# Heads gathered and gates spread by DMA in a one-core transformer block

## The chip, the cores and the metric

One core of a Trainium2 chip runs the whole block. TensorE (PE) does matmuls and transposes, VectorE (DVE), ScalarE (ACT) and GpSimd (POOL) the elementwise work, SyncE (SP) issues most transfers. The metric is the device time of one execution in microseconds (us), lower is better.

## The reference

Post-norm attention and a mixture of experts over 2 x 1024 tokens of 128 features, all in float32: 16 heads of 8 features, a rotation of queries and keys, a causal softmax, and then 4 experts of 512 hidden features, of which each token's two best are weighted by their gates.

```python
x = L0_attn_x                                    # (2, 1024, 128)
x = _layernorm(x + _L0_attn_ref(x, qw, kw, vw, ow))
x = _layernorm(x + _L0_ffn_ref(x, router_w, router_b, w1, w3, w2))
...
score = jnp.einsum('bhqd,bhkd->bhqk', Q, K) / scale      # Q, K after rope; causal mask
weights = jax.nn.softmax(score, axis=-1)
attn = jnp.einsum('bhqk,bhkd->bhqd', weights, V)
...
h = jax.nn.silu(jnp.einsum('td,edf->etf', xf, w1)) * jnp.einsum('td,edf->etf', xf, w3)
expert_out = jnp.einsum('etf,efd->etd', h, w2)
out = jnp.einsum('te,etd->td', gates, expert_out)        # gates: softmax over the top 2
```

## The kernel before

**Tiling.** Attention runs in 8 groups (2 batches x 4 groups of `GH` = 4 heads). A group has 1024 queries in `NC` = 2 halves `c` of `CH` = 512. Tokens are also cut in `CHUNKS` = 4 chunks of 512 for the second part of the block. Each group passes twice over its scores: first the 40 score units `S` (queries on partitions), whose rows DVE reduces to maxima, then the 20 units `T` (keys on partitions), which ACT exponentiates into `num`, and the 12 products `PV` with the values, which collect in `o_bank`.

**Stages.** Nine stages overlap two groups: `PROLOGUE` (projections, S of group 0), `FIRST`, six times `STEADY`, and `LAST`. Stage s does S of group s and T and PV of group s - 1. The order of units within a stage is a string written by hand (`STEADY_ORDER`, `FIRST_ORDER`): s, t, p are units, m is `MROWS`, n is `NORM`. Every engine walks the same plan in that order.

- `MROWS`: POOL splits the maxima into three bfloat16 parts, PE transposes them to rows (L1273), DVE casts the rows to `max_rows` (L973), SP sends them into `q_op` (L462). The T units of that half wait for them.
- `OCOPY`: ACT copies `o_bank` to `o_sb` (L775). Each head has 32 rows there: 8 features, the denominator, unused rows.
- `NORM`: PE transposes the copy, 4 instructions (L1283), DVE takes reciprocals of the denominators, 16 a partition (L980), and multiplies them in (L983), into `merged`.

S, MROWS and NORM share a ring of three PSUM banks (`job_bank`); the semaphore `job_read` counts what DVE has read.

**Between.** For each chunk, `between(ch, r)` has 15 steps r: `merged` is copied to `mg_w` and transposed (L1309, r = 0), copied to `mg_t`, multiplied with `wo` (L1314, r = 1), added to x (`resid`), normalised (r = 2 to 5), transposed, split in two parts, and the router's gates are worked out (r = 8 to 14). For chunk 0 these steps stand in `LAST` (the `C` steps), for the others among the experts' steps.

**Experts.** `experts(ch, n)` has a step n for each of 16 hidden tiles (4 experts x 4): PE makes both products of the tile (6 matmuls, L1338), ACT the silu, DVE the product `hid` (L1104), ACT and POOL the split into two parts, and PE multiplies tile n - 3 with w2 (3 matmuls, L1351). After each expert ACT copies the sum (`eo_sb`, L843), PE transposes it to tokens (L1360) and DVE adds it with the gate, 4 instructions (L1125). `between` of the next chunk runs at step n - `HEAD`, `HEAD` = 7. A product for tile n may start when `hid` of tile n - 2 is done. The end of the last chunk is layer norm, half of it on POOL (L668), and two stores.

**Queues.** Each engine works strictly in its written order. A wait in one step holds all that is behind it. SP's queue holds the loads and stores of `q_scratch` and `k_scratch`, the rows of maxima, weights and results; ACT's holds two loads of `k_op` in the prologue.

## Time and profile before

| | us |
|---|---|
| median of 3 runs | 411.76 (411.66 to 412.97) |
| profiled execution | 413.73 |
| its span, first to last instruction | 412.0 |
| PE / DVE / ACT / POOL busy in it | 386.8 / 310.0 / 260.8 / 208.2 |

The profile is of one execution, 1.97 us above the median, of which 1.73 us lie outside its span. The span falls into the prologue (0 to 45 us), FIRST (to 79.5), six steady stages of 25.64 us, LAST (234 to 256.7, its score-free part from 231.7), and four expert chunks of up to 37.83 us. Busy time of PE is modelled and contains waits that its pipeline hides; the chain of waits shows what PE was held by.

### The profile page before, as it was taken

The page shows a single profiled execution, that of the slowest core. Times are in us where ns is not written, and L with a number is a line of the kernel's source. Part 1 is how long each engine was busy: PE and PEld are TensorE (multiplying, and loading weights), DVE is VectorE, ACT ScalarE, POOL GpSimd, SP SyncE. Part 2 cuts the span into 40 slices and gives each one's busy share as a digit, 9 for nine tenths or more (in the row PEclk, how much of TensorE's full clock was granted, in tenths as well). Part 3 has the DMA queues.
Part 4 walks back from the last instruction along what each step waited for, and adds up shares of the span by engine and source line. Part 5 has one row for each costly group of instructions (what it writes and reads, how often), then busy time and mean ns, then how long its engine had stood idle before and what let it go on. Part 6 is the DMA issues. An engine that isn't in the chain of part 4 may idle for free.

```text
span 412.0 us, 7446 instructions
## 1 busy us (share of the span) xinstructions
PE 386.8 (94%) x2402; PEld 203.3 (49%) x2424; DVE 310.0 (75%) x1022; ACT 260.8 (63%) x373; POOL 208.2 (51%) x274
## 2 busy tenths in 40 slices
PE   6897979999999999999999998999999999999992
PEld 2441232323323233232332434888888888888780
DVE  2869799899999999999999761455586568656653
ACT  1361527686866868668686687666566756666560
POOL 7177478542614436044360422756476546755662
PEclk9996889999999999999999999999999999999997
DMA  7474011375232232322310000000000000000000
GB/s 233 160 216 95 0 22 29 88 237 173 55 94 45 47 82 55 95 45 46 85 27 3 3 1 2 0 2 1 2 1 25 2 1 27 2 0 2 25 2 25
DMA packets 46164, 21.14 MB, mean 51 GB/s; under 512 B 30379, under 2 KB 44331, under 8 KB 46126
## 3 DMA queue, kind: packets, MB, share of 16 engines
q1 hardware_dynamic: 42718, 18.44, 17.1%
q10 hardware_dynamic: 3408, 2.23, 1.8%
q8 instruction: 20, 0.33, 0.3%
q14 instruction: 18, 0.15, 0.1%
HBM read 13.11 MB, written 7.35 MB: 50 GB/s over the span
## 4 chain that ended last, share of the span: by engine, by line
PE 80%; DVE 10%; ACT 3%; issue 3%; DMA 2%; POOL 1%; POOLq 0%; SPq 0%; ACTq 0%; DVEq 0%
PE o_bank L1264 16%; PE bank L1338 11%; PE t_bank L1338 11%; PE bank L1223 10%; PE t_bank L1351 10%; PE t_bank L1246 8%; PE small_bank L1223 5%; DVE maxima L960 2%; DVE x_w L956 2%; PE o_bank L1360 2%; PE t_bank L1176 2%; ACT num L766 1%; DVE mg_w L956 1%; DMA wqk<-in_kw 1%; DVE mg_t L956 1%
## 5 line engine op out<-in xcount | busy, mean ns | idle before, releaser
L766 ACT ACTIVATE num<-t_bank 128x1024 f32<-128x1024 f32 (+2 forms) x160 | 141.9, 940 | 65.3 <-PE t_bank L1246 65.2
L659 POOL TENSOR_TENSOR hid_lo<-num,q_op 128x512 fp32r<-128x512 f32 x63 | 81.8, 1302 | 57.7 <-ACT q_op L830 56.5
L621 POOL TENSOR_SCALAR_AFFINE_SELECT num<-num 128x512 f32<-128x512 f32 x64 | 40.2, 638 | 102.2 <-ACT num L766 101.9
L1264 PE MATMUL o_bank<-num,v_op 128*32 128x512 f32 (+3 forms) x768 | 80.1, 497 | 0.1
L1223 PE MATMUL bank<-k_op,q_op 128*128 128x512 bf16 (+7 forms) x241 | 65.3, 327 | 3.4 <-DVE maxima L956 1.3
L830 ACT ACTIVATE q_op<-num 128x512 fp32r<-128x512 f32 x64 | 40.5, 632 | 42.6 <-DVE num L1104 42.1
L960 DVE TENSOR_REDUCE maxima<-bank 128x1 f32<-128x512 f32 x83 | 55.3, 684 | 2.0 <-PE bank L1223 0.8
L1246 PE MATMUL t_bank<-q_op,k_op 64*128 64x512 bf16 (+3 forms) x384 | 49.4, 334 | 3.7 <-ACT num L766 1.3
L1104 DVE TENSOR_TENSOR num<-bank,num 128x512 f32<-128x512 f32 x32 | 22.1, 691 | 34.3 <-ACT num L837 34.0
L1223 PEld LDWEIGHTS bank<-k_op,q_op 128*128 128x128 bf16 x257 | 20.7, 98 | 53.9 <-DVE maxima L960 21.8
L1104 DVE TENSOR_TENSOR num<-t_bank,num 128x512 f32<-128x512 f32 x32 | 22.1, 690 | 26.3 <-ACT num L837 24.0
L956 DVE CUSTOM_DVE_ANT_0 mg_w<-bank,resid 128x256 f32<-128x256 f32 (+7 forms) x94 | 39.4, 440 | 2.9 <-PE bank L1223 2.3
L1223 PE MATMUL small_bank<-k_op,q_op 128*128 128x512 bf16 (+7 forms) x121 | 36.8, 331 | 2.6 <-DVE maxima L960 1.0
L956 DVE CUSTOM_DVE_ANT_0 x_w<-small_bank,resid 128x384 f32<-128x384 f32 (+7 forms) x82 | 35.7, 453 | 4.1 <-PE small_bank L1223 2.7
L956 DVE CUSTOM_DVE_ANT_0 mg_t<-bank,resid 128x448 f32<-128x448 f32 (+7 forms) x80 | 35.8, 464 | 2.6 <-PE small_bank L1223 1.4
L960 DVE TENSOR_REDUCE maxima<-small_bank 128x1 f32<-128x512 f32 x45 | 30.8, 684 | 1.7 <-PE small_bank L1223 0.9
L1246 PEld LDWEIGHTS t_bank<-q_op,k_op 64*128 64x128 bf16 x384 | 14.0, 94 | 34.1 <-ACT num L766 16.2
L1264 PEld LDWEIGHTS o_bank<-num,v_op 128*32 128x32 f32 x768 | 16.0, 108 | 25.2 <-issue 21.5
L1338 PE MATMUL bank<-q_op,w_hi 128*128 128x512 f32 x64 | 26.8, 419 | 0.4 <-DVE num L1104 0.2
L1338 PE MATMUL t_bank<-q_op,w_hi 128*128 128x512 f32 x64 | 25.7, 402 | 0.0
L1351 PE MATMUL t_bank<-hid_lo,w_hi 128*128 128x512 f32 x64 | 25.4, 397 | 0.1
L1223 PEld LDWEIGHTS small_bank<-k_op,q_op 128*128 128x128 bf16 x127 | 11.0, 97 | 29.1 <-DVE maxima L960 11.2
(162 smaller groups left out, 654.6 us busy)
## 6 DMA issues: line engine op xcount, KB each, us to landing
q_op<-q_scratch SPq DMA_DIRECT2D x64, 48.0 KB
w_raw<-in_w_all SPq DMA_DIRECT2D x6, 512.0 KB, 4.0
k_op<-k_scratch SPq DMA_DIRECT2D x28, 96.0 KB, 2.2
xT<-in_x_feat SPq DMA_DIRECT2D x4, 256.0 KB, 6.0
x_res<-in_x_tok ACTq DMA_DIRECT2D x4, 256.0 KB, 3.1
q_scratch<-num SPq DMA_DIRECT2D x2, 384.0 KB, 2.8
k_scratch<-num SPq DMA_DIRECT2D x2, 384.0 KB, 2.9
out_tokens<-num SPq DMA_DIRECT2D x3, 256.0 KB, 2.3
```

The lines of the kernel that those rows point to most:

```text
L621: pool.affine_select(out=tile, in_=tile, compare_op=ALU.is_ge, fill=0.0, base=0, pattern=[[0, GH], [1, P]], channel_multiplier=-1)\
L659: pool.tensor_tensor(hid_lo[:, m % HB, :], hid[:, m % HB, :], hid_hi[:, m % HB, :].bitcast(F32), ALU.subtract).then_inc(f_lo, 1)
L766: act.activation(num[:, t % PB, :, off:CH].rearrange("p (k i) t -> p i k t", i=2)[:, :, h:h + each, :], t_bank[k % TB][:, :, 0:each * (CH ...
L830: act.activation(hid_hi[:, m % HB, :], hid[:, m % HB, :], ACT.Copy).then_inc(f_hi, 1)
L956: ins = dve.tensor_tensor_reduce(masked_s[job % SB][:, at], ring(s, step)[:, at], causal[:, CH - width:CH], 1.0, LOWEST, ALU.add, ALU.max, ...
L960: ins = dve.tensor_reduce(maxima[:, half, pr, j:j + 1], ring(s, step)[:, at], AX.X, ALU.max)
L1104: dve.tensor_tensor(hid[:, n % HB, :], bank[2 * (n % 2) + 1][:, :], silu_sb[:, n % 2, :], ALU.mult).then_inc(f_hid, 1)
L1223: ins = pe.matmul(ring(s, step)[:, i * width:(i + 1) * width], q_op[u][:, c, pr * NB + j % NB, :, :].rearrange("p i q -> p (i q)"), k_op[u ...
L1246: ins = pe.matmul(t_bank[k % TB][:, i, (pr - h) * width:(pr - h + 1) * width] .rearrange("p (j q) -> p j q", q=QB), k_op[w][rows, pr, kt * ...
L1264: ins = pe.matmul(o_bank[h * QD:(h + 1) * QD, off:CH], v_op[w][:, kt, h, :], num[:, t % PB, h, off:CH], start=kt == 0, stop=kt == TI * (c ...
L1338: ins = pe.matmul(bank[2 * (n % 2) + w][:, :], ws[:, at], xs[ch], start=k == 0, stop=k == 2)
L1351: ins = pe.matmul(bank[4 + e % 2][:, :], ws[:, at], hs[:, m % HB, :], start=f == 0 and k == 0, stop=f == FT - 1 and k == 2)
```

## The change

- **Heads.** `NORM` is gone. The value operand carries 8 columns of ones instead of one, so each head has its denominator on 8 rows. After both halves of a group, SP issues 8 transfers (`gather_heads`, 8 rows x 1024 each) that put the heads' features into `o_all` (the storage of `xT`) and the denominators into `den_all`, both with features on partitions.
- **Between, r = 0.** DVE takes the reciprocal of `den_all` (128 x 512) in place and multiplies `o_all` with it into `mg_t`. The copies to `mg_w` and `mg_t` and the transposes L1309 are gone, and so is the copy of the normalised x (`c_store`).
- **Gates.** SP writes the gates of a chunk to DRAM (4 transfers of 128 x 4 single floats) and reads them back as rows on all partitions (`gate_rows`, 128 x 4 x 512 floats). DVE multiplies each expert's sum with its row and adds it to `sum_t`, features on partitions. PE transposes once a chunk instead of after each expert. Statistics and the last normalisation read PSUM; POOL's share and ACT's copies go.
- **Rows of maxima** are cast by ACT, not DVE.
- **Order.** New strings for FIRST and STEADY. `between` of the next chunk stands at step n - 3 (`NEXT_AT`), not n - 7.
- **Prologue.** qw is loaded on SP's queue first, PE waits for each weight apart, a third warm matmul, projection 5 moved behind two scores, the sums of turned parts 2 and 3 on DVE, not POOL, the loads of `k_op` on SP, and the second half of group 1's loads behind the first rows of maxima.

```diff
-STEADY_ORDER = "ssmttssspssttsspssttsspsstspsttssspmsttsssptsspssttssspssttsspssttsspsnttnpp"
-FIRST_ORDER = "ssssmssssnsssststsstsstsssttsspssttsspmsttssspssttsspssttsspssnttppp"
+STEADY_ORDER = "sssmttssspsttssspssttsspstsstspssttsspssttsspmstsstsspssttsspsssttpssttppp"
+FIRST_ORDER = "ssssmsssssssststsstsstsssttsspssttsspmsttssspssttsspssttsspssttppp"
...
+NEXT_AT = E_LAST
+def next_steps(n, i):
+    r = n - NEXT_AT
+    return [(i + 1 + r // UNITS, r % UNITS)] if i + 1 + r // UNITS < CHUNKS else []
...
 SP:
             send_rows(0, next(step for step in PROLOGUE if step[0] == "MROWS"), 0)
+            load_q(sp, 1, 1, 1)
+            load_k(sp, 1, 1, 1)
...
+            def gather_heads(n):
+                b, g = divmod(n, NG)
+                sp.wait_ge(o_copied, 1 + NC * (n + 1))
+                for h in range(GH):
+                    for k, dst in enumerate((o_all, den_all)):
+                        at, rows = g * QD + h * DH, h * QD + k * DH
+                        sp.dma_start(dst[at:at + DH, b * S:(b + 1) * S], o_sb[rows:rows + DH, :])\
+                            .then_inc(heads_in[b], 16)
...
                         send_rows(s, step, u if step[1] == 0 else v)
+                        if step[1] == NC - 1 and n > 0:
+                            gather_heads(n - 1)
...
+            def spread_gates(ch):
+                cols = slice(ch * CH, (ch + 1) * CH)
+                sp.wait_ge(c_done, 1 + 2 * ch + 2)
+                for e in range(E):
+                    sp.dma_start(g_dram[e, cols].rearrange("(t p) -> p t", p=P),
+                                 gates[:, ch * TI:(ch + 1) * TI, e:e + 1].rearrange("p t e -> p (t e)"),
+                                 allow_slow_non_contiguous=True)\
+                        .then_inc(g_stored, 16)
+                sp.wait_ge(g_stored, 16 * E * (ch + 1))
+                sp.dma_start(gate_rows[ch % 2][:, :, :], g_dram[:, cols].partition_broadcast(P))\
+                    .then_inc(g_loaded[ch % 2], 16)
...
 ACT:
+                    if step[0] == "MROWS":
+                        _, c, use = step
+                        act.wait_ge(job_ready, JOB[n + 1, step] + 1)
+                        act.activation(max_rows[c][:, :], ring(n + 1, step)[0:NPR * PARTS * NB, 0:P], ACT.Copy)\
+                            .then_inc(rows_cast, 1)
...
+                        if g > 0 and c == 0:
+                            act.wait_ge(heads_in[(g - 1) // NG], 16 * 2 * GH * ((g - 1) % NG + 1))
+                        act.activation(o_sb[:, c * CH:(c + 1) * CH], o_bank[:, :], ACT.Copy).then_inc(o_copied, 1)
...
 DVE:
-                if first and r == 0:
-                    dve.wait_ge(job_read, SB + LAST_JOBS)
-                    dve.wait_ge(c_mgt, 1 + ch)
-                    dve.tensor_copy(mg_w[:, :].rearrange("p (i g r) -> p i g r", i=TI, g=NG),
-                                    merged[:, 1:1 + NG, 0:TI, :].rearrange("p g i r -> p i g r")).then_inc(c_mg, 1)
...
+                if r == 0:
+                    b, at = ch // NC, slice(ch * CH, (ch + 1) * CH)
+                    dve.wait_ge(heads_in[b], 16 * 2 * GH * NG)
                     dve.wait_ge(c_y, 1 + ch)
+                    dve.reciprocal(den_all[:, at], den_all[:, at]).then_inc(c_mg, 1)
+                    dve.wait_ge(c_mg, ch + 1)
+                    dve.tensor_tensor(mg_t[:, :], o_all[:, at], den_all[:, at], ALU.mult).then_inc(c_mgs, 1)
...
+                    if e == 0:
+                        dve.wait_ge(g_loaded[ch % 2], 16 * (ch // 2 + 1))
+                        dve.wait_ge(c_x1s, ch + 1)
+                    dve.wait_ge(f_w2, ch * UNITS + FT * (e + 1) + HB)
+                    for k, half in enumerate(halves(ch, e)):
+                        dve.tensor_tensor(gated[:, e % 2, half], bank[4 + e % 2][:, half], gate_rows[ch % 2][:, e, half],
+                                          ALU.mult).then_inc(f_eo, 1)
...
+                        dve.tensor_tensor(sum_t[:, half], gated[:, e % 2, half], (sum_t if e else x1_tw)[:, half],
+                                          ALU.add).then_inc(f_y, 1)
...
 PE:
-            for _ in range(WARM):
-                pe.matmul(o_bank[:, 0:CH - QB], causal[:, 0:P], causal[:, 0:CH - QB], start=True, stop=True)
+            for width in WARM:
+                pe.matmul(o_bank[:, 0:width], causal[:, 0:P], causal[:, 0:width], start=True, stop=True)
...
-                if r == 1:
-                    pe.wait_ge(c_mgs, 1 + ch + 1)
+                if r == 1:
+                    pe.wait_ge(c_mgs, ch + 1)
+                    pe.wait_ge(c_top, 1 + ch)
...
+                if n == TR_STEP:
+                    pe.wait_ge(f_z, ch + 1)
+                    for k, half in enumerate(halves(ch, E - 1)):
+                        pe.wait_ge(f_y, (ch + 1) * E + k)
```

How instructions move is shown at three places. The first is PE where a steady stage ends and the next begins, before (`bank`, `small_bank`: scores, rows or norms; `t_bank`: T; `o_bank`: PV):

```order
L1223 MATMUL small_bank<-k_op1,q_op1 128x512
L1283 MATMUL bank0<-ident,o_sb1 128x128 x4
L1246 MATMUL t_bank0<-q_op1,k_op1 128x512 x2
L1246 MATMUL t_bank1<-q_op1,k_op1 128x512 x2
L1283 MATMUL bank1<-ident,o_sb0 128x128 x4
L1264 MATMUL o_bank<-num,v_op0 32x256 x4
L1264 MATMUL o_bank<-num,v_op0 32x128 x4
L1223 MATMUL small_bank<-k_op0,q_op0 128x64 x2
L1223 MATMUL bank0<-k_op0,q_op0 128x128 x2
L1273 MATMUL bank1<-ident_b,max_part1 48x128
```

PE at the same place in the changed kernel:

```order
L1225 MATMUL bank1<-k_op1,q_op1 128x512
L1248 MATMUL t_bank0<-q_op1,k_op1 128x512 x2
L1248 MATMUL t_bank1<-q_op1,k_op1 128x512 x2
L1266 MATMUL o_bank<-num,v_op0 32x384 x4
L1266 MATMUL o_bank<-num,v_op0 32x256 x4
L1266 MATMUL o_bank<-num,v_op0 32x128 x4
L1225 MATMUL small_bank<-k_op0,q_op0 128x64 x2
L1225 MATMUL bank0<-k_op0,q_op0 128x128 x2
L1225 MATMUL bank1<-k_op0,q_op0 128x192 x2
L1277 MATMUL small_bank<-ident_b,max_part1 48x128
```

The eight transposes of `o_sb` are gone, and the rows of maxima stand one score unit later. The second place is DVE in the first expert chunk of the changed kernel, from `hid` of tile 3 on (`num<-bank1,num` and `num<-t_bank0,num` are `hid`):

```order
L1094 TENSOR_TENSOR num<-t_bank0,num 128x512
L1026 RECIPROCAL den_all<-den_all 128x512
L1028 TENSOR_TENSOR mg_t<-xT,den_all 128x512
L1094 TENSOR_TENSOR num<-bank1,num 128x512
L1031 TENSOR_TENSOR resid<-small_bank,x_res 128x512
L1094 TENSOR_TENSOR num<-t_bank0,num 128x512
```

The reciprocal and the product stand between `hid` of tile 3 and of tile 4; before, DVE had only `hid` there and a small norm. The third place is PE in the same chunk, step n = 4, in the changed kernel:

```order
L1324 MATMUL bank1<-q_op0,w_lo 128x512
L1337 MATMUL t_bank1<-q_op1,w_hi 128x512
L1337 MATMUL t_bank1<-q_op1,w_lo 128x512
L1337 MATMUL t_bank1<-hid_lo,w_hi 128x512
L1300 MATMUL small_bank<-wo,mg_t 128x128 x4
L1324 MATMUL t_bank0<-q_op0,w_hi 128x512
```

The product with `wo`, which reads `mg_t`, now stands between the matmuls of steps 4 and 5; before, it stood behind step 8, and the transposes of `mg_w` behind step 7.

## Rows read from the trace of the kernel before

**Rows 1.** The page, part 2: busy tenths in 40 slices.
```profile
PE   6897979999999999999999998999999999999992
DVE  2869799899999999999999761455586568656653
```

**Rows 2.** Table of stretches: start:end, length, busy us (instructions) by engine, granted clock.
```profile
133.18:158.82 25.64, 25.14 (x203) 8.16 (x210) 24.09 (x88) 19.34 (x24) 9.92 (x20) 1.00 0.28 65
...
288.95:326.78 37.83, 37.83 (x188) 31.11 (x186) 25.07 (x76) 24.03 (x42) 22.73 (x19) 1.00 0.03 8
```

**Rows 3.** Chain of waits, 133.18 to 158.82 us: shares, then start, length, what.
```profile
by line: PE o_bank L1264 36.1%; PE bank L1223 23.6%; PE t_bank L1246 18.2%; PE small_bank L1223 11.6%; DVE mg_w L956 2.4%; PE bank L1283 2.3%; PE small_bank L1283 1.7%; issue 1.4%; DVE max_rows L973 1.1%; PE bank L1273 0.8%; PE small_bank L
...
152.48 0.44 PE small_bank L1283 x4
...
153.46 0.59 PE bank L1283 x4
```

**Rows 4.** Instructions of DVE in order of time, same stage.
```profile
140.48 0.28 DVE L973 CAST max_rows<-small_bank 48x128 bf16<-48x128 f32 x1
...
153.40 0.25 DVE L980 RECIPROCAL rden<-small_bank 128x16 f32<-128x16 f32 x1
153.69 0.29 DVE L983 TENSOR_TENSOR merged<-small_bank,rden 128x128 f32<-128x128 f32 x1
```

**Rows 5.** Chain of waits, 288.95 to 326.78 us.
```profile
by line: PE bank L1338 29.6%; PE t_bank L1338 29.3%; PE t_bank L1351 29.3%; PE o_bank L1360 4.9%; PE small_bank L1314 2.4%; PE small_bank L1325 2.1%; PE small_bank L1309 1.5%; PE small_bank L1320 1.2%
...
306.93 0.44 PE o_bank L1360 x4
307.37 0.57 PE small_bank L1309 x4
```

**Rows 6.** Groups of instructions: line engine operation shapes xcount | busy, mean ns | idle before.
```profile
L980 DVE RECIPROCAL rden<-small_bank 128x16 f32<-128x16 f32 x8 | 2.0, 253 | 0.5 <-PE small_bank L1283 0.3
...
L1070 DVE TENSOR_TENSOR logits<-small_bank,rb 128x16 f32<-128x16 f32 x3 | 0.5, 162 | 0.0
```

**Rows 7.** Instructions of DVE in order of time, first chunk of the experts.
```profile
261.56 0.69 DVE L1104 TENSOR_TENSOR num<-t_bank,num 128x512 f32<-128x512 f32 x1 [0.70 <-ACT num L837]
```

**Rows 8.** Chain of waits around the same point.
```profile
258.34 0.44 PE small_bank L1283 x4
...
262.29 0.70 PE t_bank L1351 x3
```

**Rows 9.** Instructions of DVE at the start of the last attention stage.
```profile
230.24 0.17 DVE L966 TENSOR_TENSOR maxima<-maxima 128x16 f32<-128x16 f32 x1
```

**Rows 10.** Chain of waits, last attention stage.
```profile
233.91 1.16 PE bank L1314 x8
```

**Rows 11.** Chain of waits at the end of the kernel.
```profile
404.28 1.14 DVE num L1125 x4
...
408.93 0.79 POOL num L668
```

**Rows 12.** The page, parts 3 and 6: DMA queue and DMA issues with KB and us to landing.
```profile
q1 hardware_dynamic: 42718, 18.44, 17.1%
...
w_raw<-in_w_all SPq DMA_DIRECT2D x6, 512.0 KB, 4.0
...
x_res<-in_x_tok ACTq DMA_DIRECT2D x4, 256.0 KB, 3.1
```

**Rows 13.** Instructions of SP's queue in order of time: start, length, transfer.
```profile
36.85 1.63 SPq L462 DMA_DIRECT2D q_op<-max_rows  x2
38.52 0.43 SPq L470 DMA_DIRECT2D wo<-in_ow  x1
```

**Rows 14.** Table of stretches of 1 us; the last number but two is the granted clock.
```profile
31.00:32.00 1.00, 0.40 (x2) 0.10 (x1) 1.00 (x3) 0.74 (x2) 0.57 (x1) 1.00 1.00 192
32.00:33.00 1.00, 0.54 (x2) 0.10 (x1) 1.00 (x5) 0.00 (x0) 0.20 (x1) 1.00 0.88 143
33.00:34.00 1.00, 0.23 (x2) 0.11 (x2) 1.00 (x5) 0.00 (x0) 0.70 (x5) 1.00 0.77 169
...
35.00:36.00 1.00, 0.69 (x4) 0.18 (x3) 1.00 (x2) 0.00 (x0) 0.94 (x2) 0.50 0.34 51
...
44.00:45.00 1.00, 1.00 (x7) 0.24 (x5) 0.99 (x3) 0.75 (x1) 0.34 (x1) 0.50 0.00 0
```

374 lines of the change are left out of this document (152 added, 222 removed).

## The prediction

> **What bounds the kernel now.** I read the page's busy tenths first [rows 1]: PE stands at 9 from 25 us to the end, and DVE falls from 9 to about 5 where the experts begin. The two long parts therefore have different second limits, and I took a stretch of each [rows 2]: a steady stage has PE 25.14 and DVE 24.09 busy of 25.64 us, an expert chunk PE 37.83 of 37.83 and DVE only 25.07. Busy is not bound, so the chains come next. In the steady stage [rows 3] the shares of PE's lines add up to about 95%; DVE's `mg_w` and `max_rows` make 3.5%. In the expert chunk [rows 5] every listed share is PE's. So an instruction taken off PE pays in full in both, one taken off DVE pays in the experts nothing, and DVE may grow there by some 10 us a chunk, if it grows at a place where PE doesn't wait. The granted clock was 1.00 in both stretches.
>
> **Steady stages (6).** PE loses the transposes of `NORM`: 2.3 + 1.7 = 4.0% of 25.64 = 1.03 us a stage [rows 3]. DVE loses, for each half, the reciprocal and product (0.25 + 0.29) and the cast of the rows (0.28) [rows 4]: 1.6 us a stage; of the chain DVE had 3.5%, 0.9 us, part of which goes with it. ACT takes the casts, 2 x 0.25 (estimate from DVE's 0.28) on 19.34: no limit [rows 2]. SP gets 8 transfers, at 0.43 us an issue [rows 13] 3.4 us a stage; the next copy into `o_sb` waits for them, and has, by the written order, some 8 us. It is covered; were it not, ACT would hold T, and PE with it. Between -1.03 (PE's part alone) and -1.9 (with DVE's part of the chain) I take -1.45: **-8.7** for six. FIRST has one such stage: **-1.4**.
>
> **Prologue.** qw comes first, sums on DVE take 0.69, as for that size [rows 7], in place of a slower POOL, and SP sends the rows of maxima at 36.85, 2 us after their cast ended, behind loads [rows 13]; these now stand behind. PE is at the lower level of the clock until 45 us in any case [rows 14]. Nothing in the rows fixes what is late next: 0 to -3.5, taken **-1.5**.
>
> **LAST.** The product with `wo` of chunk 0 ran at 233.91 [rows 10], fed by merges already done; now it needs DVE's large reciprocal and product behind the join of maxima, which ends at 230.41 [rows 9]. With the price below, 3.4 + 0.7 after it is 234.5: 0.6 late. The norms are gone from the same stretch. **0** (-2 to +1.5). The norm behind the attention, 0.44 in the experts [rows 8], goes: **-0.4**.
>
> **Expert chunks, PE's part.** Of four groups of transposes of `eo_sb` a chunk one stays: 3 x 0.44 x 4 = -5.3. The transposes of `mg_w` go in chunks 1 to 3: 0.44 + 2 x 0.57 = 1.6, the row being 0.57 [rows 5]. Together **-6.9**. DVE's four weighted additions of about 1.14 [rows 11] become four pairs of 128 x 512 at about 1.3: +1. With the reciprocal and product (4.1) it comes to 28 to 30 of 36 us, and ACT falls: no bound by its share.
>
> **The large reciprocal.** This is the unknown, and the place counts. The trace has none of 128 x 512. Lower end: it costs what a product of that size does, 0.69 [rows 7]. Upper: a reciprocal of 16 elements took 253 ns, a plain operation of the same 16 from PSUM 162 [rows 6]; the 91 ns more are 5.7 ns an element, and with the 1 ns that each costs anyway it is 6.5 x 512 = 3.4 us. I take 3.4, since it is the row of the operation itself. The Trainium skill (VectorE: DVE Perf Modes, section "First, the fixed hardware budget") says that Reciprocal is an iterative divide with a repeat count of 8; at 0.96 GHz this would be an estimate of 4.3 us, and the sum below 2.5 us worse. The 253 against 162 ns point the same way.
>
> DVE starts it when `hid` of tile 3 ends, 262.25 in the first chunk [rows 7]. It delays `mg_t`, and PE now asks for `mg_t` right after the matmuls of tile 1 with w2 in step 4, which end at 262.99 [rows 8]. `mg_t` is there at 262.25 + R + 0.69 + 0.1 = 263.0 + R. So PE waits about R. `hid` of tile 4 stands behind it on DVE as well, but PE wants that only in step 6. For chunk 1 that is 3.4, for 2 and 3 (prepared in the next two chunks) 3.0 each, where PE has the late transposes of the chunk before in front of it: **+9.4**. With R = 0.69 it would be +1.5.
>
> **Gates.** The stores write 512 single floats four times: 2048 packets, 128 on each of 16 engines. The queue's packets took 0.171 x 412 x 16 / 42718 = 26 ns each, 432 bytes in the mean [rows 12]; so 3.3 us, plus four issues (1.7), some 2 for landing, and a read of 1 MB. 512 KB took 4.0 and 256 KB 3.1 [rows 12]: each doubling from there 0.9 or 1.8, so 5.8. Round trip 11 to 13 us. The gates are ready in a chunk's step 1 (r = 14 stands at n = 17), and DVE needs the rows in step 6. With steps of 2.24 us, chunk 3 has about 9.7 us, chunks 1 and 2, with the stall between, 13.5; PE stands a wait of DVE of 1.7 more. Chunk 0's stores go behind the last gather, ready at about 269 against 268.5 plus the stall. I take **+0.5** (0 to +6). A page speaks against it: the Trainium skill (DMA: Bandwidth & Descriptors, section "Rules for kernel authors") says that a non-contiguous last dimension becomes one descriptor for each element and should be made contiguous. The packet count above is its rule; that single floats cost more than 432 bytes no row here shows.
>
> **Tail.** The last additions (1.14) and POOL's 0.79 with its 0.88 of the other half [rows 11] give way to shorter halves on DVE, against one copy more in the chain: **-1.3** (-0.5 to -1.5).
>
> **Sum.** -1.5 - 1.4 - 8.7 + 0 - 0.4 - 6.9 + 9.4 + 0.5 - 1.3 = -10.3. The profiled execution, 413.73 (span 412.0 and 1.73 outside it), becomes 403.4. The median lies 1.97 below it, so it becomes 401.5.
>
> **Rivals.**
> - A, the reciprocal costs about 1 ns an element like the rest. For: DVE's operations of that size took 0.69. Against: 253 against 162 ns at 16 elements. The stalls fall from 9.4 to 1.5, and LAST gains up to 2: 391 to 393.5. Chance 0.18.
> - B, the stalls cost the clock. For: PE was busy 1.17 of 3 us from 31 to 34 us at granted 1.00 and then stood at 0.50, the 1.2 GHz level, until 45 [rows 14]. A stall of 3.0 to 3.4 us of nothing is alike. If some 3 us of work then run at half speed, each of three stalls costs 1.5 more: 406. Against: around the stall PE is full, as it wasn't there. Chance 0.17. Were the low level held 10 us each time, it would be +15 and the gain gone; I count a tenth of B so.
> - C, the one on the slower side: gates late. DVE waits for `gate_rows` in step 6 with `hid` of the next tiles behind, and PE stands. With a round trip T the chunks 1 to 3 lose 3T - (2 x 15.2 + 11.4); the gain of the other terms, 10.8, is gone at 3T = 52.6, T = 17.5 us. Issue, landing and reload make 9.5, so this decides from 62 ns a packet, 2.4 times the 26 ns. At four times (104 ns) T is 22.8 and chunk 0 is late too: +27 and about +5, 433. For: 4-byte packets, which the trace doesn't have in number; against: 2.4 times is far from a mean of 432 bytes, and moving fewer bytes shouldn't be dearer. Chance 0.07.
> - D, it doesn't do what it says in the steady stages: PE's 1.03 us come back as waits, since DVE's 24.09 less 1.6 and ACT's 19.8 must fit another order with three banks. Half the gain: -4.4 instead of -8.7, 406. For: DVE is near; against: it loses more than PE. Chance 0.08.
>
> **How the numbers follow.** The forecast has 0.5: 401.5, its own range 398 to 404.5 from R at 4.3 us or at 2.5, the prologue's 0 to -3.5 and the steady -1.03 to -1.9. The range to hold 8 in 10 reaches from A with its end, 391, to B and D with 2 us above them, 408; outside lie C and the heavy part of B, and the ends of the prologue and LAST on both sides. A measurement can tell about 0.3%, 1.2 us. Faster by more than that: forecast, A, most of B and D, 0.87; slower: C and little of B, 0.08; within: what lies between, 0.05.
>
> **What would show it.** Steady stages at 24.2 us (25.6 - 1.45), with PE's share near 98%; a row of the reciprocal of 128 x 512 with 3.4 us (0.7 gives A); PE idle about 3 us before the product with `wo` in step 4 of the first three chunks; chunks of 36 us where no such stall is (the last); granted clock 1.00 behind the stalls (0.5 gives B); from the first gate store to the landing of `gate_rows` 11 to 13 us and no wait of DVE for it (a wait gives C); the gathers of heads landed before ACT's copy of the next group asks for them; 1.3 us less after the last matmul. The forecast is wrong if the reciprocal is cheap, if PE's waits grow as its work shrinks, or if the single floats take more than 60 ns each.

## The result and the profile after

The changed kernel takes 567.14 us (median of 4 runs, 564.83 to 570.15), the kernel before 411.76: a ratio of 1.377 (95% interval 1.369 to 1.385). The forecast was 401.5, with a range of 391 to 408. The sign is wrong, and by far: 155 us slower.

The page of the changed kernel, part 2 (span 563.8 us, 14.1 us a slice), against [rows 1]:

```profile
PE   7878999899999999797505975008882059840094
DVE  5788989889898989535105672025670065510245
PEclk9978999999999999898856999557997578985578
```

Up to the 18th digit it looks like before. Then there are four holes, one in each expert chunk, where no engine works, and PEclk falls with them. Next a table of three stretches that both kernels have, between ACT's copies of `o_bank`: the six steady stages, the last attention stage, and all from the last copy on. First the kernel before, then the changed one (start:end, length, busy us and instructions of PE, PEld, DVE, ACT, POOL, granted clock, DMA share, GB/s):

```profile
78.06:232.04 153.98, 150.82 (x1194) 49.12 (x1211) 144.83 (x523) 116.13 (x140) 59.65 (x121) 1.00 0.29 74
232.04:253.34 21.30, 19.56 (x171) 7.22 (x171) 11.17 (x39) 16.49 (x23) 6.72 (x10) 1.00 0.01 2
253.34:412.00 158.66, 150.09 (x716) 122.18 (x716) 93.63 (x271) 94.76 (x165) 90.37 (x72) 0.98 0.03 8
```

```profile
75.02:227.24 152.22, 144.93 (x1146) 44.81 (x1161) 136.50 (x487) 120.56 (x152) 59.10 (x121) 1.00 0.37 86
227.24:251.17 23.93, 19.44 (x162) 7.00 (x161) 12.09 (x34) 16.59 (x23) 6.88 (x12) 0.93 0.08 13
251.17:563.80 312.63, 159.83 (x652) 123.38 (x652) 114.47 (x247) 81.53 (x139) 92.61 (x70) 0.77 0.11 18
```

The steady stages gained 1.8 us, the last stage lost 2.6, the part before 78.06 gained 3.0 (75.02). The attention as a whole is 2.2 us shorter. The experts are 154 us longer. The waits of this part name most of it (who waited for whom: us, times, longest):

```profile
DVE num L1110 <- DMA num<-gate_scratch: 68.2, 2, 36.0
DVE num L1110 <- DMA turns_sb<-gate_scratch: 57.8, 2, 30.4
```

DVE waited 126.0 us for the rows of gates. One such round, for chunk 1, on SP's queue (start, length, transfers), and then the table of stretches over the same time:

```profile
329.60 2.01 SPq L534 DMA_DIRECT2D gate_scratch<-gates  x4
365.42 0.36 SPq L539 DMA_DIRECT2D num<-gate_scratch  x1
```

```profile
330.00:333.00 3.00, 2.41 (x14) 1.76 (x12) 2.57 (x5) 1.42 (x3) 2.36 (x2) 1.00 0.35 3
333.00:340.00 7.00, 5.21 (x28) 4.15 (x27) 5.95 (x9) 2.24 (x4) 3.14 (x3) 1.00 0.00 0
340.00:364.00 24.00, 6.52 (x29) 4.95 (x27) 2.61 (x11) 2.58 (x5) 2.27 (x2) 0.71 0.00 0
...
366.00:376.00 10.00, 0.00 (x0) 0.00 (x0) 0.64 (x1) 0.00 (x0) 0.00 (x0) 0.50 0.43 105
```

The four stores were issued by 331.61, their packets ran from 330 to 333 (DMA share 0.35), and then no packet of anything ran until 366 (share 0.00); SP's queue, which would have issued the next ones, stood in the wait. SP waited for the stores to count as landed until 365.42, 33.8 us after the last issue, and the load landed another 10 us later. The packets' own time says nothing of it. In the four chunks the wait was 29.0, 33.8, 31.8 and 34.2 us.

### The profile page after: what moved, and what is told of

Its sections match the earlier page's. It is cut to its first block, busy times and chain, and to the rows that moved or that the text cites. A ratio compares the mean times of both kernels' runs of the same rounds, so it can differ in the third digit from the quotient of the medians.

```text
span 563.8 us, 7129 instructions
## 1 busy us (share of the span) xinstructions
PE 387.2 (69%) x2272; PEld 198.7 (35%) x2294; DVE 322.8 (57%) x952; ACT 252.8 (45%) x363; POOL 206.5 (37%) x268
## 2 busy tenths in 40 slices
DMA packets 57746, 27.43 MB, mean 49 GB/s; under 512 B 39403, under 2 KB 53355, under 8 KB 57710
## 4 chain that ended last, share of the span: by engine, by line
PE 35%; issue 25%; DVE 13%; DMA 11%; SPq 7%; ACT 5%; POOL 4%; POOLq 0%; DVEq 0%; ACTq 0%
PE o_bank L1266 7%; DMA gate_scratch<-gates 6%; PE bank L1225 6%; PE t_bank L1248 5%; PE bank L1324 4%; PE t_bank L1324 4%; PE t_bank L1337 3%; POOL hid_lo L693 3%; PE small_bank L1225 3%; DVE den_all L1026 2%; DVE num L1094 2%; DMA num<-gate_scratch 2%; ACT num L853 2%; SPq L494 2%; SPq L450 2%
## 5 line engine op out<-in xcount | busy, mean ns | idle before, releaser
L977 DVE TENSOR_REDUCE maxima<-bank 128x1 f32<-128x512 f32 x108 | 70.8, 683 | 3.0 <-remote 1.7
L1225 PE MATMUL bank<-k_op,q_op 128*128 128x512 bf16 (+6 forms) x226 | 66.3, 346 | 3.9 <-DVE maxima L977 1.4
L1324 PEld LDWEIGHTS t_bank<-q_op,w_hi 128*128 128x128 f32 x64 | 13.6, 212 | 136.5 <-DVE num L1094 133.1
L973 DVE CUSTOM_DVE_ANT_0 x_w<-small_bank,resid 128x64 f32<-128x64 f32 (+7 forms) x116 | 43.6, 401 | 9.9 <-PE bank L1225 6.4
L1094 DVE TENSOR_TENSOR num<-bank,num 128x512 f32<-128x512 f32 x32 | 22.1, 690 | 43.5 <-ACT num L853 39.4
L1110 DVE TENSOR_TENSOR num<-t_bank,num 128x512 f32<-128x512 f32 (+1 forms) x9 | 5.5, 625 | 68.8 <-DMA num<-gate_scratch 68.2
L973 DVE CUSTOM_DVE_ANT_0 x_tw<-bank,resid 128x256 f32<-128x256 f32 (+7 forms) x76 | 34.9, 477 | 7.4 <-PE bank L1225 5.9
L1225 PE MATMUL small_bank<-k_op,q_op 128*128 128x64 bf16 (+7 forms) x136 | 33.7, 293 | 3.7 <-ACT num L789 1.0
L1094 DVE TENSOR_TENSOR num<-t_bank,num 128x512 f32<-128x512 f32 x32 | 22.0, 689 | 24.1 <-ACT num L853 21.3
L973 DVE CUSTOM_DVE_ANT_0 mg_t<-bank,resid 128x320 f32<-128x320 f32 (+4 forms) x64 | 32.5, 518 | 1.7 <-PE bank L1225 0.3
L1324 PE MATMUL t_bank<-k_op,w_hi 128*128 128x512 f32 x64 | 27.8, 435 | 0.0
L1324 PE MATMUL t_bank<-q_op,w_lo 128*128 128x512 f32 x64 | 27.8, 434 | 0.0
```

The lines of the kernel that those rows point to most:

```text
L973: ins = dve.tensor_tensor_reduce(masked_s[job % SB][:, at], ring(s, step)[:, at], causal[:, CH - width:CH], 1.0, LOWEST, ALU.add, ALU.max, ...
L977: ins = dve.tensor_reduce(maxima[:, half, pr, j:j + 1], ring(s, step)[:, at], AX.X, ALU.max)
L1094: dve.tensor_tensor(hid[:, n % HB, :], bank[2 * (n % 2) + 1][:, :], silu_sb[:, n % 2, :], ALU.mult).then_inc(f_hid, 1)
L1225: ins = pe.matmul(ring(s, step)[:, i * width:(i + 1) * width], q_op[u][:, c, pr * NB + j % NB, :, :].rearrange("p i q -> p (i q)"), k_op[u ...
L1324: ins = pe.matmul(bank[2 * (n % 2) + w][:, :], ws[:, at], xs[ch], start=k == 0, stop=k == 2)
```

## What each experiment showed

All of them start from the changed kernel. Each median is given with that of the kernel before on the same chip. g_half, g_far, g_64, g_pe, no_recip, two_o and cast_dve have one execution each, `placed` and `placed2` twelve, the others four. g_half, g_far, g_64 and no_recip leave out values or mix them up, as their texts say.

| kernel | us | before | what it is |
|---|---|---|---|
| g_half | 497.1 | 413.8 | half the single floats |
| g_far | 442.0 | 413.8 | floats 512 bytes apart |
| g_64 | 438.4 | 413.2 | floats 64 bytes apart |
| g_pe | 450.2 | 413.8 | gates turned by PE, whole rows stored |
| g_pe4 | 447.4 | 413.8 | the same, loaded in four |
| no_recip | 441.3 | 413.0 | g_pe4, no reciprocal |
| next7 | 447.1 | 413.0 | g_pe4, `between` at n - 7 |
| two_o | 442.6 | 413.0 | g_pe4, two `o_sb` |
| cast_dve | 450.7 | 413.0 | g_pe4, rows cast by DVE |
| old_exp | 431.2 | 413.3 | old experts, changed attention |
| spread | 428.8 | 413.3 | old_exp, reciprocal in quarters |
| spread2 | 424.3 | 413.3 | spread, two `o_sb` |
| placed | 412.2 | 413.2 | spread2, quarters moved |
| placed_new | 433.3 | 413.2 | placed, changed experts |
| placed2 | 413.0 | 412.6 | placed, quarters moved again |

### The single floats

**g_half.**

```diff
-                for e in range(E):
+                for e in range(2):
                     sp.dma_start(g_dram[e, cols].rearrange("(t p) -> p t", p=P), ...
...
-                sp.dma_start(gate_rows[ch % 2][:, :, :], g_dram[:, cols].partition_broadcast(P))
+                for k in range(2):
+                    sp.dma_start(gate_rows[ch % 2][:, 2 * k:2 * k + 2, :], g_dram[0:2, cols].partition_broadcast(P))
```

> The changed kernel, but the gates of two experts only are stored, 1024 single floats a chunk and not 2048, and their rows are read twice, so that as much is loaded (the gates of experts 2 and 3 are those of 0 and 1). In the changed kernel the packets of the stores are over 3 us after the issue, and SP still waits some 32 us until they count as landed. Theory 'each element': the wait is a price per 4-byte element, some 15 ns each one after the other; it halves to 15 to 17 us and the kernel takes about 500 to 505 us. Rival 'fixed': the wait doesn't depend on their number; 32 us again, 567 us.

**g_far and g_64.**

```diff
+        g_far = nc.dram_tensor("gate_far", (E, T, P), F32).ap()      # g_64: (E, T, 16)
-                    sp.dma_start(g_dram[e, cols].rearrange("(t p) -> p t", p=P), ...
+                    sp.dma_start(g_far[e, cols, 0:1].rearrange("(t p) x -> p (t x)", p=P), ...
```

> The changed kernel, but each of the 2048 single floats of a chunk goes to a line of its own, 512 bytes apart in DRAM; what is read back is stored beside it in whole 64-byte rows, in the order of the SBUF (so tokens get gates of others). Theory 'shared line': neighbouring 4-byte writes into one line of DRAM wait for each other; apart, they land 2 to 5 us after the last packet, and the kernel takes about 420 to 430 us. Rival 'each element': the price belongs to the element wherever it goes; 30 us or more again, about 567 us.

> g_far with the single floats 64 bytes apart, not 512. If what waits is a line of 64 bytes or less, as g_far: SP's wait 1.4 us, 442 us. If the unit is larger (up to 512 bytes, 8 of these floats), a wait of 3 to 20 us remains and the time is 450 to 500 us.

SP's queue in the three, for chunk 1: g_half, then g_far, then g_64.

```profile
311.17 0.91 SPq L534 DMA_DIRECT2D gate_scratch<-gates  x2
329.64 0.87 SPq L540 DMA_DIRECT2D num<-gate_scratch  x2
```

```profile
305.95 2.02 SPq L535 DMA_DIRECT2D gate_far<-gates  x4
308.01 0.50 SPq L539 DMA_DIRECT2D gate_scratch<-gates  x1
310.11 0.33 SPq L542 DMA_DIRECT2D num<-gate_scratch  x1
```

```profile
303.93 2.03 SPq L535 DMA_DIRECT2D gate_far<-gates  x4
306.00 0.51 SPq L539 DMA_DIRECT2D gate_scratch<-gates  x1
308.20 0.33 SPq L542 DMA_DIRECT2D num<-gate_scratch  x1
```

With half the floats SP waited 17.6 us (329.64 - 312.08) where it was 33.8: 17.2 and 16.5 ns a float, as if one went after the other (13.9 to 18.7 us over the four chunks of g_half). With all 2048 floats 512 bytes apart it waited 1.6 us (310.11 - 308.51), 64 bytes apart 1.7 (1.5 to 1.6 and 1.3 to 2.3 over the chunks). So the number of 4-byte packets is harmless, and their neighbourhood is not: "each element" holds for floats side by side and "fixed" falls, and "shared line" is right, with a line of 64 bytes or less. That neighbours wait for each other in DRAM is the reading that fits all three; the memory itself is in no trace. The kernel's time of g_far missed its text (420 to 430 us), since the gates were not all that was wrong.

**g_pe and g_pe4.**

```diff
+                if n == 2:                                   # PE
+                    pe.wait_ge(c_done, 1 + 2 * ch + 2)
+                    pe.transpose(small_bank[0:TI * E, 0:P], gates[:, ch, :, :].rearrange("p e t -> p (e t)"), ident[:, :])
+                if n == 2:                                   # ACT
+                    act.activation(gate_t[:, :], small_bank[0:TI * E, 0:P], ACT.Copy).then_inc(g_copied, 1)
-                for e in range(E):                           # SP
-                    sp.dma_start(g_dram[e, cols].rearrange("(t p) -> p t", p=P), ...
+                sp.dma_start(g_dram[ch, :, :].rearrange("e (t p) -> (e t) p", p=P), gate_t[:, :]).then_inc(g_stored, 16)
+                for e in range(E):                           # g_pe4 only; one load in g_pe
+                    sp.dma_start(gate_rows[ch % 2][:, e, :], g_dram[ch, e, :].partition_broadcast(P))
```

> The changed kernel with the gates turned by one PE transpose of 128x16 and one copy by ACT a chunk, stored as 16 rows of 512 bytes, read back as before by one load of 1 MB. If the single floats are all that is wrong with the round trip, store to load takes 2 to 3 us in place of 32 and the load 10 us as in the changed kernel; DVE waits at most 2 us a chunk for it, and the time is 415 to 419 us: the experts of before (158.7 us from the last copy of o_bank) with 6.9 off and three stalls of 3.4 plus 1 to 2 of low clock on, behind an attention 2.2 us earlier. Rival: the read of 1 MB by 128 partitions is itself late, with waits of 4 us or more a chunk: 425 us or more.

> As g_pe, but the rows come in four loads of 256 KB, one for each expert with a semaphore of its own, so that the first expert's row is there some 7 us earlier. DVE should wait for no row. If the waits of g_pe were 1 to 2 us a chunk and hidden by PE's slack, 415 to 418 us, within 2 us of g_pe; slower than before by about 1%, from the large reciprocals alone.

Store to load fell to 1.05 us (g_pe4: store 306.00 0.32, loads from 307.37), DVE waits for no gate, and 120 us of the 155 are gone (567.1 to 447.4). The load changed too. These are the rows of the same 1 MB in the changed kernel and in g_pe:

```profile
turns_sb<-gate_scratch SPq DMA_DIRECT2D x2, 1024.0 KB, 10.0
```

```profile
turns_sb<-gate_scratch SPq DMA_DIRECT2D x2, 1024.0 KB, 4.7
```

In g_pe, as in g_far and g_64 (4.7 to 6.1 us), each partition reads one piece of 8 KB, and the changed kernel reads four rows of 2 KB that lie 8 KB apart. So 10.0 us isn't the price of 1 MB; whether the layout or the stores before it made it so, no run separates.

But both are at 447 to 450, not 415 to 419 as expected: some 34 us over the kernel before remain without any wait for a transfer. The product with `wo` (L1300 in the changed kernel) of two chunks comes 48.2 and 49.6 us apart, before 37.8.

### The other 34 us

The part from ACT's last copy of `o_bank` to the end of the span, in one trace of each kernel (us; PE's busy time is modelled):

| kernel | length | PE busy | PE idle | granted clock |
|---|---|---|---|---|
| before | 158.7 | 150.1 | 8.6 | 0.98 |
| g_pe4 | 193.3 | 156.5 | 36.8 | 0.94 |
| two_o | 189.4 | 152.5 | 36.8 | 0.96 |
| no_recip | 183.7 | 153.2 | 30.5 | 0.95 |
| old_exp | 175.8 | 153.7 | 22.1 | 0.95 |
| spread2 | 171.7 | 154.8 | 16.9 | 0.94 |
| placed | 160.1 | 149.1 | 11.0 | 0.98 |
| placed_new | 178.4 | 150.7 | 27.7 | 0.97 |

g_pe4's 34.6 us over the kernel before are 28.2 of waiting and 6.4 of matmuls that take longer, though there are fewer of them: that is the lower clock behind the waits, as spread2 and placed show with the same instructions.

PE's waits in one chunk of g_pe4 (start, length, instruction, and in brackets the idle time before it and its releaser):

```profile
305.40 0.27 PE L1322 MATMUL small_bank<-ident,gates 128*16 128x128 f32 x1 [1.88 <-DVE gates L1086]
314.52 1.16 PE L1302 MATMUL small_bank<-wo,mg_t 128*128 128x128 f32 x8 [1.87 <-DVE mg_t L1029]
329.11 0.66 PE L1308 MATMUL small_bank<-ident,x_w 128*128 128x128 f32 x4 [2.46 <-DVE x_w L1009]
336.26 1.05 PE L1313 MATMUL small_bank<-rw,x_tw 128*128 128x4 f32 x8 [0.78 <-ACT x_tw L831]
```

With 1.42 and 0.29 us for `hid` they make 8.7 us, where the kernel before had none [rows 5]. The first is my own, from the place of the transpose; the others are of the changed kernel, which shows 3.26, 1.79 and 1.78 us at its product with `wo`, 0.6 at `x_w` and 1.2 at `x_tw` beside its holes. DVE in the same chunk:

```profile
307.78 0.69 DVE L1095 TENSOR_TENSOR num<-bank,num 128x512 f32<-128x512 f32 x1 [2.52 <-ACT num L854]
308.39 0.68 DVE L1111 TENSOR_TENSOR num<-t_bank,turns_sb 128x512 f32<-128x512 f32 x1
309.10 0.69 DVE L1117 TENSOR_TENSOR num<-num 128x512 f32<-128x512 f32 x1
309.79 0.69 DVE L1095 TENSOR_TENSOR num<-t_bank,num 128x512 f32<-128x512 f32 x1
310.40 3.34 DVE L1027 RECIPROCAL den_all<-den_all 128x512 f32<-128x512 f32 x1
313.77 0.69 DVE L1029 TENSOR_TENSOR mg_t<-xT,den_all 128x512 f32<-128x512 f32 x1
314.38 0.68 DVE L1095 TENSOR_TENSOR num<-bank,num 128x512 f32<-128x512 f32 x1
314.98 0.88 DVE L1124 BATCH_NORM_STATS2 y_stats<-o_bank 128x6 f32<-128x128 f32 x4
315.78 0.68 DVE L1032 TENSOR_TENSOR resid<-small_bank,x_res 128x512 f32<-128x512 f32 x1
```

From 307.78 to 316.5 DVE has no gap, though it is busy only 28.3 of the 40 us from 290 to 330. The end of one chunk (sums, statistics, normalisation) and the start of the next (reciprocal, product, residual) meet here.

**no_recip and next7.** The first leaves the division out.

```diff
-                    dve.reciprocal(den_all[:, at], den_all[:, at]).then_inc(c_mg, 1)      # no_recip
-                    dve.wait_ge(c_mg, ch + 1)
...
-NEXT_AT = E_LAST                                                                          # next7
+NEXT_AT = HEAD
+SUM_AT = {10: 0, 12: 1, 14: 2, EO_STEP + 12: 3}
```

> g_pe4 without the reciprocals (o_all is multiplied by the sums themselves; the division is left out). In g_pe4 the rows of the gates are on time and yet an expert chunk takes 49 us (before 38): from step 3 on DVE has the reciprocal, then the additions, statistics and normalisation of the chunk before and of the chunk after in one stretch, and PE waits up to step 9 for hid. Theory 'pile': the reciprocal is the largest piece of the pile, not all of it; without it each chunk is 5 to 7 us shorter, 42 to 44 us, the last attention stage 3, and the time 425 to 430 us. Rival 'reciprocal alone' (with the low clock behind its stalls): chunks of 36 to 37 us, the time about 405 us.

> g_pe4 with the steps between chunks at step n - 7 again, behind the end of the chunk before (as in the kernel before), and the weighted sums of experts 0 and 1 at steps 10 and 12, since the gates come four steps later. Reciprocals stay. Theory 'pile': DVE's work no longer meets; the chunk falls from 49 to about 40 us (36 of matmuls, 3 to 4 for the reciprocal), the time to 420 to 425 us. Rival 'reciprocal alone': it stalls PE at step 8 as much as at step 4, 445 us or more.

Neither theory 'pile' got its number; next7 came out at its rival's (445 or more), and no_recip at none. Without the reciprocals 6 us are gained, not 17 to 40. In the traces it is 7.6: 9.6 behind the last copy, less 2.0 in the attention, 1.5 of them in LAST, where ACT's copy now waited 2.58 us for the gather. The waits at `gates` (1.88), `x_w` (2.46), `x_tw` (1.45) and `hid` (1.42) are all still there. With the steps moved nothing is gained; PE waits 2.64 us at the product and 2.24 at `x_w`, at their new places. The reciprocal alone is not the cause, and the distance of the two groups of steps alone isn't either. What was left to change was the form of the experts, and the reciprocal's own place.

**two_o and cast_dve**, for the steady stages.

```diff
-        o_sb = sb("o_sb", [P, S])                                         # two_o
+        o_two = [sb(f"o_sb{i}", [P, S]) for i in range(2)]
...
+                    if step[0] == "MROWS":                                # cast_dve, on DVE, not ACT
+                        dve.tensor_copy(max_rows[step[1]][:, :], ring(s, step)[0:NPR * PARTS * NB, 0:P])
```

> g_pe4 with two buffers for the copy of o_bank, so that ACT's copy doesn't wait for the gather of the group before. In the changed kernel that copy waited 0.2 to 1.2 us in each steady stage, and the stages took 24.9 us where it was 0.2 and 25.5 to 26.0 where it was more. If the gather is the cause, all six stages take 24.7 to 24.9 us and the attention ends 2 to 3 us earlier. Rival: the longer stages are those with other transfers or splits, and stay at 25.5 to 26.0 us.

> g_pe4 with the rows of maxima cast by DVE again. ACT was idle 0.8 us a stage before its casts, waiting for PE, with the next exponentials behind. If moving the cast to ACT cost PE its exponentials, the stages get 0.3 to 0.5 us shorter (24.5 in place of 24.9); if it helped, since DVE is the second limit, 0.3 to 0.5 us longer. Theory: no difference above 0.3 us a stage, so it isn't what kept the stage from 24.2.

Two stages of the changed kernel in the table of stretches, and ACT's copy in each:

```profile
101.94:127.90 25.96, 24.36 (x193) 7.46 (x195) 22.84 (x84) 20.16 (x25) 9.41 (x20) 1.00 0.39 82
152.84:177.78 24.94, 24.04 (x193) 7.54 (x196) 22.66 (x82) 20.07 (x26) 9.85 (x21) 1.00 0.34 75
```

```profile
112.12 0.60 ACT L805 ACTIVATE o_sb<-o_bank 128x512 f32<-128x512 f32 x1 [1.18 <-DMA den_all<-o_sb]
...
161.93 0.60 ACT L805 ACTIVATE o_sb<-o_bank 128x512 f32<-128x512 f32 x1 [0.18 <-DMA den_all<-o_sb]
```

With two buffers the second to the sixth stage took 24.90 to 24.95 us each, the first 26.30; six together 151.0, in g_pe4 152.3. So the wait for the gather cost 1.3 us in the steady stages, not 2 to 3, and the long first stage has another cause, left open. (The whole kernel was 4.8 us faster than g_pe4 by one execution. In the traces it is 5.8 us. Of these 1.9 lie in the attention, and 3.9 among the experts, whose code is the same: PE is idle there for 36.8 us in both, but busy 4 us less, at a granted clock of 0.96 against 0.94. So that part is the clock and not the second buffer; why it was higher stays open.) The cast on DVE makes a stage 25.1 to 25.2 in place of 24.94: as the theory said, it isn't what kept the stage from 24.2.

**old_exp, spread, spread2.** The changed attention with the experts of the kernel before; then the reciprocal in quarters; then with two buffers.

```diff
-                    dve.reciprocal(den_all[:, at], den_all[:, at]).then_inc(c_mg, 1)      # spread
+            def invert(ch, k):
+                part = slice(ch * CH + k * P, ch * CH + (k + 1) * P)
+                dve.reciprocal(den_all[:, part], den_all[:, part]).then_inc(c_mg, 1)
...
+                        if s in (GROUPS - 2, GROUPS - 1) and done in (10, 26):
+                            invert(0, 2 * (s - GROUPS + 2) + (done == 26))
...
+                if n in (3, 4, 5, 6) and ch + 1 < CHUNKS:
+                    invert(ch + 1, n - 3)
```

> The changed attention (heads gathered, new orders, rows cast by ACT, large reciprocals) with the experts of the kernel before: no gates to DRAM, each expert's sum copied by ACT, turned by PE, added by DVE, and the steps between chunks at n - 7. g_pe4 and next7 took 447 us with all rows on time. Theory 'experts': the weighting on features costs most of their 35 us, because DVE's two 128x512 operations and the normalisation stand in front of hid and of x1; with the old experts the chunk is 38 us less the old transposes (1.6) plus the stall at the large reciprocal (2.6 and some low clock): 416 to 420 us. Rival 'reciprocal and clock': the stalls at the reciprocal with the low clock behind them are the cause; then 440 us or more.

> old_exp with each reciprocal of 128x512 cut in four of 128x128 (0.84 us each): those of chunk 0 among the scores of the last two steady stages, those of the next chunk in its steps 3 to 6. The product waits for nothing long. If the stalls (3.0, then 2.6 three times, low clock behind) are what old_exp loses, this gives 10 to 13 us: 404 to 408 us, faster than before by 1 to 2%. Rival: the quarters delay hid or the scores by as much and PE waits there; 415 us or more.

> spread with two buffers for the copy of o_bank. In two_o the steady stages all took 24.94 us and the attention was 1.3 us shorter by it. 1 to 2 us less than spread: 403 to 406 us.

The old form of the experts is worth 16 us against next7 (447.1 to 431.2), which has the same steps between chunks. Both theories of old_exp missed: it lies between them, since the experts' form and the reciprocal's place both count. The quarters gave 2.4 us, not 10 to 13, as spread's rival had it (415 or more). The second buffer then gave 4.6 us, not 1 to 2: in spread ACT's copy in LAST waited 2.51 us for the gather, and LAST fell from 24.0 to 20.9 us with it. PE's longest wait moved little, from 5.0 us in old_exp to 3.8 in spread2:

```profile
319.25 1.95 PE L1316 MATMUL small_bank<-wo,mg_t 128*128 128x128 f32 x8 [5.03 <-DVE mg_t L1042]
```

```profile
312.09 2.07 PE L1327 MATMUL small_bank<-wo,mg_t 128*128 128x128 f32 x8 [3.80 <-DVE mg_t L1051]
```

DVE in front of the latter (spread2, in order of time) is again without a gap:

```profile
305.02 0.69 DVE L1118 TENSOR_TENSOR num<-bank,num 128x512 f32<-128x512 f32 x1
305.63 0.94 DVE L975 RECIPROCAL den_all<-den_all 128x128 f32<-128x128 f32 x1
306.49 2.40 DVE L1031 TENSOR_SCALAR num<-num,y_mv,y_rstd 128x128 f32<-128x128 f32 x4
308.81 0.68 DVE L1118 TENSOR_TENSOR num<-t_bank,num 128x512 f32<-128x512 f32 x1
309.41 1.11 DVE L1139 SCALAR_TENSOR_TENSOR num<-o_bank,gates,x 128x128 f32<-128x128 f32 x4
310.44 1.59 DVE L1051 TENSOR_TENSOR mg_t<-xT,den_all 128x512 f32<-128x512 f32 x1
```

**placed, placed_new, placed2.** The quarters go where DVE had gaps.

```diff
+INVERT_AT, MERGE_AT = {9: 0, 10: 1, 13: 2, 14: 3}, 1          # placed2: {13: (0, 1), 14: (2,), 17: (3,)}, 2
...
+                if n in INVERT_AT and ch + 2 < CHUNKS:
+                    invert(ch + 2, INVERT_AT[n])
+                if n == MERGE_AT and ch + 1 < CHUNKS:
+                    merge(ch + 1)                              # mg_t = o_all * den_all
...
+                        if step[1] == 0:                       # step E 0, in LAST
+                            for k in range(TI):
+                                invert(1, k)
```

> spread2 with the quarters of the reciprocals and the product with them moved out of steps 3 to 7, where DVE had no gap: those of chunks 2 and 3 to steps 9, 10, 13 and 14 two chunks ahead, those of chunk 1 in front of the experts, where DVE idles 6 us, the products to step 1. spread2 still lost 0.8 + 3.8 + 3.8 us at the product with wo and 6.8 us of low clock behind each of the last two. Theory 'pile': DVE's work stood in a row there, whatever its share of the chunk; now PE waits for nothing in the chunks, they take 36.5 to 37 us (before 37.9), and the time is 407 to 411 us, same as before or faster by up to 1%. Rival: the waits move to other steps, 418 us or more.

> placed with the changed kernel's experts (weighting on features, gates turned by PE at step 7 and loaded in four parts, sums at 10, 12, 14, 18) in place of the old. PE has 1.3 us less work a chunk than in placed, DVE 1 us more. Theory: the experts' new form costs by its place too; with two 128x512 operations of DVE in front of x1's normalisation PE waits 2 us at step 13 and 1 to 2 us at step 15, with low clock behind: 412 to 420 us, slower than placed by 1 to 2%. Rival: with the reciprocals out of the way it wins what it takes off PE, 3 to 5 us less than placed.

> placed with the quarters at steps 13 (two), 14 and 1 and the product at step 2, none beside the statistics of x1 at steps 9 and 10. In placed PE still waited 1.0 us for x_w and 0.3 us for x_tw in each of two chunks, and the product with wo came every 39.1 us (before 37.8). Theory 'place': without quarters in front of x_w, whose four instructions took 2.5 us there and 1.1 before, the chunks take 36.5 to 37.5 us and the time is 1.5 to 4 us less than placed, 408 to 411 us. Rival: DVE has no room at steps 1 and 2 either and the wait moves, 412 us or more.

placed takes 412.17 us, 0.997 of the kernel before (0.995 to 1.000): as good as the same, and 12 us better than spread2 with the same instructions in other steps. It is just outside the 407 to 411 us of "pile", but the comparison settles the cause: it was the place. By the table above, half of the 12 us is waiting (PE idle 16.9, then 11.0) and half the clock, which stays at 0.98 where PE doesn't wait (PE busy 154.8, then 149.1). One of its chunks in the table of stretches, product with `wo` to product with `wo`:

```profile
269.44:308.52 39.08, 37.76 (x182) 30.66 (x181) 30.10 (x76) 21.85 (x39) 21.66 (x18) 1.00 0.00 1
```

DVE is busy 30 to 31 of 39 us and PE waits 1.3. My expected 36.5 to 37 us was too low by my own rows: a chunk of 37.8 loses only the 0.57 of the transposes of `mg_w` [rows 5], and 37.3 plus 1.3 is 38.6. In placed2 the wait for `x_w` is gone and one of 1.42 us for `hid` stands in its stead; the chunks take 39.4 and the time is the same as before (1.001, 0.999 to 1.004). So the rival held there: with 30 us of work DVE has no free place left.

placed_new gets the changed experts back and takes 433.3 us, 21 more than placed (expected 0 to 8 more), though PE has 1.3 us less to do a chunk. Its waits in one chunk:

```profile
283.23 0.66 PE L1329 MATMUL small_bank<-ident,x_w 128*128 128x128 f32 x4 [2.25 <-DVE x_w L1030]
...
290.54 1.05 PE L1334 MATMUL small_bank<-rw,x_tw 128*128 128x4 f32 x8 [2.48 <-ACT x_tw L833]
...
301.34 0.63 PE L1373 MATMUL o_bank<-ident,num 128*128 128x128 f32 x4 [1.34 <-DVE num L1138]
```

With 0.9 at the product with w2, 0.66 for `hid` and 0.2 for the gates they are 7.8 us. No gate is late. In front of `x_w` DVE has an expert's sum (279.47 to 281.2) and no reciprocal; in front of `k_op`, the lower part of x1 (289.13), it has a quarter (0.94 us) and a sum (1.8 us). In the third chunk no quarter runs, and the wait for `x_w` is the same, 2.23 us, while that for `x_tw` is 0.77. So the wait for `x_w` comes from the sum in front of it, with x_w's own four instructions at 2.05 us in place of 1.1, and the wait for `x_tw` mostly from a quarter that meets a sum. The pair placed and placed_new shows the 21 us for the whole new form, but placed_new has its sums at steps 10 and 12, not at 6 and 10 as the changed kernel, so they are of this arrangement.

## Where the prediction was wrong, and where not

**Gates, forecast +0.5, measured +120** (after against g_pe4). This is the step that failed most. It priced a single float at 26 ns, the mean of packets of 432 bytes [rows 12], and dismissed more with "moving fewer bytes shouldn't be dearer". The packets' own time was no dearer: they were over in 3 us at a DMA share of 0.35, about 8 ns each (3 x 0.35 x 16 / 2048). What was missed is what comes behind them: 33.8 us until they count as landed. That is 16.5 ns a float one after the other, or 264 ns in the prediction's count of 128 on each of 16 engines, where it took 26 and named 60 as the sign of being wrong. The load's 5.8 us were exceeded here (10.0) and kept in g_pe (4.7). Rival C had the mechanism and its place right (DVE at e = 0, `hid` behind it), but a chance of 0.07 and an end of 433; its threshold of 17.5 us counts on a gain of 10.8 that never came, so nothing tests it. The rule of the Trainium skill that the prediction cited (DMA: Bandwidth & Descriptors, section "Rules for kernel authors") speaks against such a transfer without a price, and I let a price from the wrong rows overrule it. The traces agree with its count and its advice: g_pe has 8384 packets under 512 bytes fewer than the changed kernel, and the single floats are 8192. But g_far has as many of them as the changed kernel (39979 against 39403) and waits 1.6 us, so the count isn't what costs.

**"No bound by its share".** The second failed step, behind most of the other 34 us: DVE "28 to 30 of 36 us" in a chunk was nearly right (30.1 of 39.1 in placed), and the conclusion wrong. The work stood in a row in steps 3 to 8. old_exp, spread2 and placed take the reciprocal of the same elements, old_exp in one piece and with one buffer for the copy, and need 431.2, 424.3 and 412.2 us. The -6.9 of PE's part of the chunks was never seen by itself, since PE waits in every run with the new experts.

**The large reciprocal, forecast 3.4 us, measured 3.34** (128 x 128 took 0.94 in the median, not the 0.84 that spread's text has). The value scaled from rows of 16 elements held, and the estimate of 4.3 worked out from the Trainium skill (VectorE: DVE Perf Modes, section "First, the fixed hardware budget") was too high. PE's waits at the product, forecast 3.4, 3.0, 3.0, were 3.26, 1.79 and 1.78. So rival A fell.

**The clock (rival B, 0.17): its mechanism came true.** In LAST PE idled 1.89 us before the product, in the first chunk 3.26, and both times the granted clock then stood at 0.50, the 1.2 GHz level:

```profile
231.00:232.00 1.00, 1.00 (x5) 1.00 (x6) 0.00 (x0) 0.00 (x0) 0.32 (x1) 0.50 0.23 33
...
265.00:266.00 1.00, 1.00 (x5) 0.90 (x5) 0.37 (x1) 0.33 (x1) 0.59 (x1) 0.50 0.00 0
```

The eight matmuls of the product took 2.08 us in LAST and 1.16 before [rows 10]. Over its whole span g_pe4 had a mean clock of 0.950 against 0.977 before, and its matmuls among the experts took at least 6.4 us longer, where rival B had 4.5. It wasn't only the three stalls of rival B: the clock fell behind other waits too.

**Steady stages, forecast -8.7, measured -1.8.** PE's busy time fell as reckoned, from 25.14 [rows 2] to 24.04, but an undisturbed stage fell only from 25.64 to 24.94. The waits of PE in it grew from 0.5 to 0.9 us, so DVE's part of the chain, which I had half cashed in, didn't go; that is rival D, and six such stages would make its -4.4 (-4.2). A gather's issues took 0.62 to 0.70 us each, not 0.43, 5.4 us a stage, and ACT's copy waited for them, which two_o prices at 1.3 us in the steady stages. "It is covered" was wrong by that. The long first stage, 26.3 even in two_o, takes about as much again.

**LAST, forecast 0, measured +2.6**: product 4.5 us after the join of maxima (226.40 to 230.88), as worked out (4.1); missed were the T units behind it on PE, with ACT idle 4.5 us, and the clock. Without the large reciprocal in it and with two buffers (spread2, placed) LAST took 20.9 and 21.0 us, before 21.3.

**Right:** the tail from the last matmul with w2 on, -0.85 (-1.3, within its bounds). **Not shown:** prologue -1.7 (forecast -1.5) and FIRST -1.4 (-1.4) fit, but by luck as far as the runs tell. The first copy of `o_bank` stood at 48.02, before at 49.68, each in one trace, and the later runs, with the same prologue, have it anywhere from 47.4 to 50.3. FIRST took 27.0 to 28.0 us in them, before 28.4.

## What to carry to other kernels

Before single elements are stored side by side by DMA, turn them on PE and store whole rows: one transpose and one copy (0.3 us each) replaced 33.8 us. Or keep them 64 bytes apart (1.7 us); reading such floats back wasn't tried. A duration taken from long packets is no bound for short ones, and a store's price is read at who waits for its landing, not at its packets. When an edit adds work to an engine that is not the bound, look at the stretch in which it lands, item by item, in front of what another engine asks for: the share of the chunk said 77%, and moving the same instructions was worth 12 us, half of it in clock.
